# A fused attention and expert kernel: 29 instead of 17 expert tiles in the first part, and what is ordered around the hand-over

## The reference

```python
# x: [16, 512, 128] f32, 16 heads of width 8
q, k, v, gate = (x @ W.T).reshape(16, 512, 16, 8)          # one weight each
beta, alpha = sigmoid(x @ Wb.T), exp(-exp(A_log) * softplus(x @ Wa.T + dt_bias))
# gated delta rule over the 512 time steps, state S [8, 8] per head
S = S * a_t;  delta = (v_t - k_t S) * beta_t;  S = S + k_t outer delta;  y_t = q_t S
x1 = layernorm(x + (rmsnorm(y, norm_w) * silu(gate)) @ Wo.T + bo)
# mixture of experts on the 8192 tokens of x1
e = argmax(x1 @ router_w.T)                                # one of 8 experts a token
ffn = (silu(x1 @ gate_w[e].T) * (x1 @ up_w[e].T)) @ down_w[e].T   # inner width 352
out = layernorm(x1 + ffn)
```

## Time and profile before

| what | value |
|---|---|
| executions, median (range) | 782.53 us (780.32 to 783.58) |
| profiled execution | span 785.4 us; this is the only time recorded for it |
| TensorE | busy 84%, mean granted clock 0.909 |
| VectorE, GpSimd, ScalarE | busy 81%, 77%, 53% |
| chain that ended last | TensorE 33%, VectorE 32%, GpSimd 17%, issue 7% |
| attention ends, first expert tile's matmuls | about 587 us |
| last expert tile's matmuls end | 767.6 us |

### The profile page before, as it was taken

The page is one execution under the profiler, slowest core; times in us unless marked ns, Lnnn a source line. Parts: engine busy times, 40 slices in busy tenths (PEclk is TensorE's granted clock), DMA queues, the critical chain, the costliest instruction groups (busy, mean ns, idle before and its releaser), DMA issues.

```text
span 785.4 us, 13851 instructions
## 1 busy us (share of the span) xinstructions
PE 659.5 (84%) x3513; PEld 502.7 (64%) x3513; DVE 632.3 (81%) x1701; ACT 415.3 (53%) x1313; POOL 601.7 (77%) x758
## 2 busy tenths in 40 slices
PE   8778699898989889999998978576689878999980
PEld 3445374755747556574654746465579778999980
DVE  3899999999999999999999999996953525666430
ACT  6736455656566546655556566233224335666651
POOL 2888797989999999999999999996733354444673
PEclk9879798989999999898999999788759989999996
DMA  6833233351433416333262432217254456677630
GB/s 172 198 95 97 65 101 87 80 151 53 128 102 89 129 54 148 92 100 96 83 155 64 116 91 74 71 37 268 67 176 150 148 179 203 230 239 235 212 116 5
DMA packets 135919, 97.28 MB, mean 124 GB/s; under 512 B 95630, under 2 KB 110225, under 8 KB 135714
## 3 DMA queue, kind: packets, MB, share of 16 engines
q1 hardware_dynamic: 130514, 87.55, 38.7%
q0 software_dynamic: 4320, 8.43, 3.3%
q10 hardware_dynamic: 1008, 0.43, 0.2%
HBM read 39.80 MB, written 31.43 MB: 91 GB/s over the span
## 4 chain that ended last, share of the span: by engine, by line
PE 33%; DVE 32%; POOL 17%; issue 7%; ACT 6%; DMA 1%; another core or an unknown queue 1%; DVEq 0%; ACTq 0%; POOLq 0%
PE banks L434 11%; DVE banks L1903 6%; PE banks L447 5%; DVE banks L1877 5%; DVE upd L1891 5%; POOL q_prod L1308 4%; DVE prod L1861 4%; DVE banks L1887 3%; DVE mix L1881 3%; PE banks L750 3%; POOL u L1308 2%; DVE upd L1872 2%; PE banks L674 2%; POOL solve L1308 2%; POOL x_sorted L346 2%
## 5 line engine op out<-in xcount | busy, mean ns | idle before, releaser
L1308 POOL TENSOR_TENSOR q_prod<-s_keep,q_gam 128x512 f32<-128x512 f32 x128 | 140.7, 1100 | 16.5 <-ACT s_keep L1006 9.0
L1006 ACT ACTIVATE s_keep<-banks 128x128 f32<-128x128 f32 x128 | 50.3, 393 | 170.1 <-DVE upd L1891 164.1
L750 PE MATMUL banks<-q_prod,ident 128*128 128x240 f32 (+1 forms) x496 | 113.7, 384 | 20.8 <-POOL q_prod L1308 20.7
L750 PEld LDWEIGHTS banks<-q_prod,ident 128*128 128x128 f32 x496 | 94.6, 195 | 41.2 <-POOL q_prod L1308 30.3
L434 PE MATMUL banks<-xs_t,w_tile 128*128 128x128 f32 x852 | 111.6, 282 | 8.6 <-issue 5.1
L543 POOL DMA_INDIRECT out<-rows_out,xs x71 | 70.1, 987 | 60.3 <-ACT rows_out L524 51.6
L1903 DVE TENSOR_REDUCE banks<-upd 128x128 f32<-128x640 f32 x128 | 105.7, 826 | 7.4 <-DVE upd L1891 0.5
L434 PEld LDWEIGHTS banks<-xs_t,w_tile 128*128 128x128 f32 x852 | 104.8, 198 | 10.3 <-issue 7.5
L578 DVE TENSOR_TENSOR hid<-banks,silu 128x384 f32<-128x384 f32 x71 | 39.6, 557 | 71.9 <-PE banks L434 39.6
L1877 DVE TENSOR_REDUCE banks<-prod 128x64 f32<-128x576 f32 x128 | 93.7, 732 | 0.0
L1861 DVE TENSOR_TENSOR prod<-banks,k_gam 128x512 f32<-128x512 f32 x128 | 88.3, 690 | 3.4
(11 more groups left out here) (224 smaller groups left out, 1481.1 us busy)
## 6 DMA issues: line engine op xcount, KB each, us to landing
w_tile<-gate_up_we SPq DMA_DIRECT2D x71, 352.0 KB
xs<-x_sorted SPq DMA_DIRECT2D x71, 64.5 KB, 1.9
x_ct<-in_x_ct SPq DMA_DIRECT2D x16, 256.0 KB, 2.9
k_dram<-kq_s SPq DMA_DIRECT2D x16, 256.0 KB, 2.9
q_dram<-kq_s SPq DMA_DIRECT2D x16, 256.0 KB, 3.8
out<-v_s SPq DMA_DIRECT2D x16, 256.0 KB, 2.6
out<-beta SPq DMA_DIRECT2D x16, 256.0 KB, 3.5
k_h<-k_dram SPq DMA_DIRECT2D x16, 256.0 KB, 3.3
```

Of the source, the lines that this page charges most:

```text
L750: i = mm(out, ident[:, :], q_prod[m][:, d, :, 1 - m:], start=(m == 0 and d == 0), stop=(d == DH - 1), skip_group_check=True)
L1308: b.step(label, win, lambda: tt(out, x, y, op))
```

## The change

Part one grows to 29 tiles (WA = 9). Tiles `xs` and `res2` that lay in memory the attention doesn't use stay 17 (`KEPT`), and so do the steps of the normalisation; the rows of tiles 17 to 28 are loaded behind a wait for the attention's last matmul. The region fills move ahead of the weights of tile 13. In part two rows run four tiles ahead of the weights issued beside them instead of one. `table_b` runs in nine pieces of two, ahead of steps 6 to 14. Small things in PSUM move to make room for the wider first table.

```diff
-WA = 6
+WA = 9
 TA = -(-(WA * TW * P - E * (P - 1)) // P)
...
+        KEPT = 17
+        FILL_AT, AHEAD = 13, 4
...
-        xs = [sb(f"xs{n}", [P, D + 1]) for n in range(TA)]
+        xs = [sb(f"xs{n}", [P, D + 1]) for n in range(KEPT)]
...
+        SIDE = 392
...
         def finish_sync(eng):
 
             fill_regions(eng)
-            for tile in range(TA, TA + NG - 1):
+            for tile in range(FILL_AT, TA):
                 load_weights(eng, tile)
             eng.wait_ge(s_sorted, 16 * (NT - WA * TW))
             eng.wait_ge(s_pad, 16 * (1 + E))
-            for tile in range(TA, TA + NG):
+            for tile in range(TA, TA + AHEAD):
                 load_rows(eng, tile)
             for tile in range(TA, NF):
-                if tile + NG < NF:
-                    load_rows(eng, tile + NG)
-                if tile + NG - 1 < NF:
-                    load_weights(eng, tile + NG - 1)
+                load_weights(eng, tile)
+                if tile + AHEAD < NF:
+                    load_rows(eng, tile + AHEAD)
...
-        mid = list(range(TA - 4, NF - 18, 3))
+        mid = list(range(KEPT - 4, NF - 18, 3))
...
-        n_newton, NORM = 11, TA - 3
+        n_newton, NORM = 11, KEPT - 3
...
             for n, step in enumerate(range(DVE_TAIL, NF + 1)):
-                if n < 3:
-                    table_b(eng, 6 * n, 6 * n + 6)
+                if n < 9:
+                    table_b(eng, 2 * n, 2 * n + 2)
...
-                for tile in range(NG + 2, TA):
+                for tile in range(NG + 2, KEPT):
                     load_rows(e, tile)
-                for tile in range(NG, TA):
+                for tile in range(NG, FILL_AT - 2):
+                    load_weights(e, tile)
+                b.wait(pe, "attn", p)
+                for tile in range(KEPT, TA):
+                    load_rows(e, tile)
+                for tile in range(FILL_AT - 2, FILL_AT):
                     load_weights(e, tile)
                 return
```

More of the change, by code:

```diff
@@ L192, in block_kernel @@
         var2, rstd2, newton = sb("var2", [P, NF]), sb("rstd2", [P, NF]), sb("newton", [P, 3])
-        xs = [sb(f"xs{n}", [P, D + 1]) for n in range(TA)]
-        res2 = [sb(f"res2_{n}", [P, D + 1]) for n in range(TA)]
-        xs += [sb(f"xs{n}", [P, D + 1]) for n in range(TA, NR)]
-        res2 += [sb(f"res2_{n}", [P, D + 1]) for n in range(TA, NV)]
+        xs = [sb(f"xs{n}", [P, D + 1]) for n in range(KEPT)]
+        res2 = [sb(f"res2_{n}", [P, D + 1]) for n in range(KEPT)]
+        xs += [sb(f"xs{n}", [P, D + 1]) for n in range(KEPT, NR)]
+        res2 += [sb(f"res2_{n}", [P, D + 1]) for n in range(KEPT, NV)]
         rows_out = [sb(f"rows_out{n}", [P, D]) for n in range(NO)]
         side = pre_ps[:, 2, :]
-        tail_cand, tail_before = (side[:, n:n + TW * E].rearrange("p (t e) -> p t e", e=E) for n in (2 * P, 2 * P + TW * E))
-        tail_top, tail_place = side[:, 3 * P:3 * P + TW], side[:, 3 * P + TW:3 * P + 2 * TW]
-        down_mean = side[:, 3 * P + 2 * TW:3 * P + 2 * TW + IC * E]
+        SIDE = 392
+        tail_cand, tail_before = (side[:, n:n + TW * E].rearrange("p (t e) -> p t e", e=E) for n in (SIDE, SIDE + TW * E))
+        tail_top, tail_place = (side[:, n:n + TW] for n in (SIDE + 2 * TW * E, SIDE + 2 * TW * E + TW))
+        down_mean = side[:, SIDE + 80:SIDE + 80 + IC * E]
         cand, before = (chain_ps[n][:, 2 * P:2 * P + TW * E].rearrange("p (t e) -> p t e", e=E) for n in range(2))
@@ L475, in expert_act @@
                 A(silu[tile % 2][:, :], g_ps(tile)[:, 0:IC * P], ACT.Silu).then_inc(s_silu, 1)
-        mid = list(range(TA - 4, NF - 18, 3))
+        mid = list(range(KEPT - 4, NF - 18, 3))
         last = mid[-1]
-        ends = [(0, TA - 4), (last, last + 3)] + [(a, a + 2) for a in range(last + 3, NF - 2, 2)] + [(NF - 2, NF - 1), (NF - 1, NF)]
+        ends = [(0, KEPT - 4), (last, last + 3)] + [(a, a + 2) for a in range(last + 3, NF - 2, 2)] + [(NF - 2, NF - 1), (NF - 1, NF)]
         mids = list(zip(mid, mid[1:]))
-        n_newton, NORM = 11, TA - 3
+        n_newton, NORM = 11, KEPT - 3
         def normed(step):
@@ L582, in finish_dve @@
             v = nc.vector
-            for n in range(TA, NV):
+            for n in range(KEPT, NV):
                 v.memset(res2[n][:, D:D + 1], (LN_EPS * D) ** 0.5)
             for n, step in enumerate(range(DVE_TAIL, NF + 1)):
-                if n < 3:
-                    table_b(eng, 6 * n, 6 * n + 6)
+                if n < 9:
+                    table_b(eng, 2 * n, 2 * n + 2)
                 expert_dve(eng, step)
@@ L594, in pads @@
                 v.memset(w_tile[n][:, 2 * I:I + IC * P], 0.0).then_inc(s_wpad, 1)
-            for n in range(TA):
+            for n in range(KEPT):
                 v.memset(res2[n][:, D:D + 1], (LN_EPS * D) ** 0.5)
```

## The result

| what | before | after |
|---|---|---|
| executions, median (range), 20 each | 781.43 us (777.43 to 784.06) | 776.75 us (773.49 to 780.59) |
| ratio, 95% interval | | 0.9937 (0.9922 to 0.9952) |
| span of the profiled execution | 785.4 us | 773.8 us |
| TensorE busy, mean granted clock | 84%, 0.909 | 85%, 0.914 |

The change takes 4.7 us or 0.6% off. The two profiles shown are 11.6 us apart, more than twice that. In the later runs an execution's own time stands 1.8 us above its span (783.72 beside 781.9, 778.99 beside 777.2), so the profiled execution of the kernel before took some 787.2 us, longer than any of the twenty. So its rows need a second witness, and the experiments give one.

A forecast was written before the change was run, and what follows sets the result against it. The expert stage was taken as bound by TensorE with a hole in it, 15.2 us lost between tiles 8 and 18. Terms +0.5 - 2.9 + 0.5 - 4.9 + 0.5 = -6.3 us, off 782.53, gave 776.2; range 771 to 781.

The forecast's parts named there:

- First table, +0.5: VectorE's serial chain in the last attention window: five operations growing from 136 to 232 elements add 0.5 us, unhidden.
- Tiles 8 to 13, -2.9: Expert stage: part two's table in nine pieces starts tile 13 at 627.2, just behind its weights, 2.9 us earlier.
- the unnamed wait of the profile shown: Ahead of tile 9 in the kernel before: a 2.41 us stretch ending with nothing the profile names.
- the 0.9 us charged to the later pieces: Table pieces after the first exceed their free 0.34 us each, adding 0.9 us up to tile 13.
- The estimate of 2.5 us: Tile 13's weights, issued by SyncE at 623.9, land 2.5 us later, at 626.4.
- Tiles 13 to 15, +0.5: Expert stage: half of the later table pieces' second 0.9 us falls by tile 15, adding 0.5 us.
- Tiles 15 to 18, -4.9: Hand-over: tile 17's row wait goes, ScalarE's eight scaled tiles bind; 10.9 us instead of 15.8, gaining 4.9.
- The half clock's 1.7 us: Hand-over: the gap behind ScalarE's scaled tiles is followed by one tile at half clock, costing 1.7 us.
- the unnamed stretch: Hand-over: 6.78 us ending with nothing named; the rival that it stays adds 2.5 us, giving 778.7, chance 0.2.
- Single banks, tiles 18 to 28, +0.5: These tiles, in single PSUM banks with `rows_out`, lose 0.5 us together, between 0 and 3.
- the rival on the slower side: Tiles 17 to 28 fall to half clock, +1.7 us each, +20.4 in all: 796.6 us, chance 0.08.
- Part two, 0: From tile 29 on: rows asked for five tiles ahead of use, no change; at worst one landing time, 1.9 us.

The follow-up runs named there:

- the second profile of the one before: The kernel before, run and profiled again with no edit: 783.72 us, span 781.9 us.
- The run with three pieces: The changed kernel with part two's table in three pieces of six again, ahead of steps 6, 7 and 8: 780.1 us, ratio 0.9981.
- the run with the fills late: The changed kernel with the region fills behind the weights of tile 28 instead of ahead of tile 13's: 783.04 us, ratio 1.0019.
- the second profiles: Both kernels run and profiled again with no edit: 783.72 us for the kernel before, 778.99 us for the changed kernel.
- the spread run: The changed kernel with ScalarE's burst of eight scaled tiles spread, none until step 16, then two a step: 774.41 us, ratio 0.9910.

## Why the prediction was right, and where it was off

From a median of three executions 776.2 us was forecast; 776.75 was measured, inside the range. The forecast gain was 6.3 us and the measured one is 4.7; that the two times lie closer than the two gains is luck, since the three executions ran 1.1 us above the median of all twenty. Step by step, the changed kernel against the second profile of the one before:

- **First table, +0.5.** Five operations grew by 0.10 us each, as worked out. That nothing hides them isn't shown: they can't be seen in the start of the first tile, which varies by 8 us.
- **Tiles 8 to 13, -2.9.** -3.1 (14.8 to 11.7). The run with three pieces confirms the mechanism, and its price is right too: the three pieces exceed their 0.34 us of play by 4.0 us together, and in the second profile of the kernel before tile 13 comes 4.2 us behind the steady pace. But the working had 1.6 us too much in the total before, the unnamed wait of the profile shown, and 1.8 too much in the total after. Part of the latter are the 0.9 us charged to the later pieces up to tile 13. They aren't there: in the run with the fills late the tiles beside them keep to 2.12 us. In their place stand 0.6 us in which tile 13 is late behind its weights. The estimate of 2.5 us from the issue of weights to their use held: 622.77 to 625.39, less TensorE's own start. That tile 13 would start just behind its weights was right too, with 12 to 13 at 2.7 us.
- **Tiles 13 to 15, +0.5.** +0.3, but not through pieces of the table, as forecast: with the fills late the same pieces leave 4.24 us. It comes behind the late weights of 13 (13 to 14 takes 2.4).
- **Tiles 15 to 18, -4.9: the step that failed, as a size.** What it said of the changed kernel came out nearly to the tenth: 10.9 forecast, 10.8 and 11.1 measured, with a wait of 2.7 us behind ScalarE and then one tile of 3.78 us near half clock (0.55). But it was set against 15.8 us from the one profile, where the kernel usually takes 12.8. Measured between the second profiles the term is -2.0, outside the bounds given for it. The half clock's 1.7 us in it agree with what the tile took (3.78 and 3.50 instead of 2.12), but by luck: they were read from tile 9 to 10, which takes 3.52 us behind the same piece of the table at full clock as well. The smaller of these bounds (-2.4) took the unnamed stretch as something that might stay in the kernel after; the other reading, that it isn't usual in the kernel before, was not weighed, though the span of that profile already stood above all three executions.
- **Single banks, tiles 18 to 28, +0.5.** Nothing: 2.12 us a tile at a granted clock of 1.00, with `rows_out`. With it falls the rival on the slower side. The Trainium skill's "TensorE: Matmul & The Clock Gate", section "A second HAM failure mode: psum-queue depth-cycling", had spoken for that rival; no tile here shows it. (The gap ahead of tile 9, which the prediction puts down in favour of this rule, was the unnamed wait, and nothing ties it to banks.) The same page reports in "HAM oscillation — how this bites in real kernels" that double-buffering in PSUM brought its kernel nothing further, and with that the trace agrees: 2.12 us with one bank and with two.
- **Part two, 0.** 0.3 us more from 18 to 70, and 0.9 us less from tile 70 to the end, which the prediction doesn't have. The end is 21.3 to 21.4 us in every kernel with 29 tiles and, but for the odd first profile, 22.3 to 22.4 in every one with 17. The difference lies behind the last instruction in the trace, GpSimd's last scatter: from its end to the end of the span it is 9.3 to 9.4 us with 17 tiles, the first profile included, and 8.4 with 29. So it is not the experts' work; its cause stays open.

Together: 0.5 + 0.2 (tiles 0 to 8) - 3.1 + 0.3 - 2.0 + 0.3 - 0.9 = -4.7 us. That this meets the measured gain to the tenth is luck too: with the first profile of the changed kernel in place of the second, the same sum gives some 2 us.

## What to carry to other kernels

Compare a profile's span with the executions' times before using it as a base: here it lay above them all, and the waits that nothing in it named stood in that one profile only. Ask of each stall what else is late at the same place: the wait for rows and the burst on ScalarE stood side by side, so taking the first away was worth 1 us with the second there and 4 without. And cutting a job into smaller pieces also makes it end later: nine pieces alone made the kernel slower, since the table's readers waited, until the order behind the table was changed with them.

## What the runs showed of the hardware that was not expected

- An idle of 2.35 + 0.36 us on TensorE was followed by a granted clock of 0.55 (3.78 us for the next tile), and one of 2.40 us in the run with the fills late by 0.60. One of 1.97 us in the spread run was not (clock 1.00, the next tile took 2.44), and neither were 0.3 + 0.4 us.
- GpSimd's `pow` of 13 columns took 2.47 us and held ScalarE 2.2 us; ten scaled tiles in a row took ScalarE 3.02 us, of which TensorE felt 1.1.
- The time at which the attention ends differed by 7.8 us between executions whose attention differed by at most half a microsecond of work. It goes with the whole time: in the nine edited kernels with a median, the profiled execution lay 4.5 us below its kernel's median where the first tile started at 585.2, within 1.2 of it from 589.0 to 590.4, and 2.4 to 4.9 above it from 591.8 to 593.0. So this, more than the expert stage, makes the spread of the times. What moves it stays open.
